# Local masked scores on alternating PSUM banks with the mask laid a unit ahead, local products on one bank, routing weights stored by one DMA

## The reference, cut to what matters

```python
x = L0_attn_x                                   # (8, 1024, 256)
xn = _layernorm(x)
return x + attn(xn) + ffn(xn)
# attn: 16 heads of 16; heads 0-3 causal ("global"), heads 4-15 causal inside a
#       window of 64 ("local"): scores, -inf where masked, softmax, times v, out projection
# ffn:  two branches (fwd, inv), each 8 experts of rank 64:
xV = einsum('btd,kdr->btkr', Q_side, V);  cum_yW = cumsum(einsum('btd,kdr->btkr', K_side, W))
weights = softmax(gelu(Q_side @ router_w1.T + b1) @ router_w2.T + b2 + expert_bias)
out = einsum('btkr,kdr->btd', xV * cum_yW * weights[..., None], U) + weights @ b
```

## Time and profile before, and how to read them

| | us |
|---|---|
| median of 3 runs | 1487.91 (1486.12 to 1490.52) |
| the profiled execution's own time | 1491.34 |
| its span | 1489.6 |
| PE busy | 1379.5 (93%) |
| DVE busy | 989.5 (66%) |
| ACT busy | 776.1 (52%) |
| POOL busy | 586.5 (39%) |

### The profile page before, as it was taken

One profiled execution on the slowest core, in us unless ns is written; L12 is line 12 of the kernel. 1 busy time (PEld: TensorE's weight loads), 2 busy tenths in 40 slices (PEclk: granted clock), 3 DMA queues, 4 the chain that ended last, 5 costly groups with the idle time before them and its releaser, 6 DMA issues.

```text
span 1489.6 us, 35980 instructions
## 1 busy us (share of the span) xinstructions
PE 1379.5 (93%) x14481; PEld 1035.7 (70%) x14481; DVE 989.5 (66%) x2082; ACT 776.1 (52%) x1368; POOL 586.5 (39%) x663
## 2 busy tenths in 40 slices
PE   5978999999999999999999999999999999999996
PEld 4567685777758677586856778587775868667773
DVE  6667777567756777557875677566875578656661
ACT  2434537455464735645374554646356453755544
POOL 1025343453514444253433525144452534335341
PEclk9999999999999999999999999999999999999998
DMA  8430625326062541616353171624516153431610
GB/s 189 102 94 11 168 79 127 105 65 174 25 175 70 121 126 49 166 32 151 96 123 107 40 196 30 158 87 107 141 42 163 44 146 100 118 109 42 172 40 15
DMA packets 166614, 152.88 MB, mean 103 GB/s; under 512 B 37809, under 2 KB 149808, under 8 KB 166448
## 3 DMA queue, kind: packets, MB, share of 16 engines
q1 hardware_dynamic: 166448, 150.59, 38.8%
HBM read 108.57 MB, written 35.65 MB: 97 GB/s over the span
## 4 chain that ended last, share of the span: by engine, by line
PE 62%; DVE 15%; ACT 8%; issue 6%; DMA 4%; POOL 2%; SPq 1%; ACTq 0%; POOLq 0%; DVEq 0%
PE PS L676 30%; PE PS L787 11%; PE PS L821 4%; DVE rest L1193 3%; PE PS L880 3%; ACT HE L1063 3%; PE PS L807 3%; PE PS L909 3%; PE PS L898 2%; PE PS L963 2%; DMA weights_d<-weights_t 2%; DVE area L1198 2%; DVE area L1196 2%; ACT HE L1055 2%; ACT PS L1048 1%
## 5 line engine op out<-in xcount | busy, mean ns | idle before, releaser
L1504 POOL TENSOR_TENSOR PL<-prod,PH 128x512 fp32r<-128x512 f32 x128 | 164.7, 1287 | 201.3 <-ACT PH L1037 201.3
L676 PE MATMUL PS<-XH,WH 128*128 128x512 f32 x512 | 218.6, 427 | 21.7 <-ACT prod L1027 10.3
L1037 ACT ACTIVATE PH<-prod 128x512 fp32r<-128x512 f32 x128 | 80.8, 632 | 268.8 <-DVE prod L1305 252.8
L1499 POOL TENSOR_TENSOR prod<-prod,rest 128x512 f32<-128x512 f32 x96 | 124.8, 1303 | 242.9 <-DMA rest<-weights_d 166.6
L1229 DVE TENSOR_REDUCE block_peak<-PS 128x4 f32<-128x512 f32 x288 | 179.8, 685 | 48.0 <-PE PS L821 47.9
L676 PE MATMUL PS<-XH,WL 128*128 128x512 f32 x512 | 204.1, 399 | 0.0
L676 PE MATMUL PS<-XL,WH 128*128 128x512 f32 x512 | 203.6, 398 | 0.0
L1482 POOL TENSOR_SCALAR_AFFINE_SELECT HE<-HE 128x256 f32<-128x256 f32 x128 | 51.2, 406 | 364.2 <-ACT HE L1063 360.6
L1063 ACT ACTIVATE HE<-PS 128x512 f32<-128x512 f32 (+1 forms) x320 | 159.9, 553 | 33.5 <-PE PS L880 30.5
L1305 DVE TENSOR_TENSOR prod<-PS,prod 128x512 f32<-128x512 f32 x128 | 87.8, 686 | 97.3 <-PE PS L676 84.5
L676 PEld LDWEIGHTS PS<-XH,WH 128*128 128x128 f32 x512 | 97.1, 190 | 63.2 <-ACT prod L1027 16.8
(11 more groups left out here) (186 smaller groups left out, 3064.6 us busy)
## 6 DMA issues: line engine op xcount, KB each, us to landing
parts_d<-area SPq DMA_DIRECT2D x32, 768.0 KB, 5.0
area<-parts_d SPq DMA_DIRECT2D x128, 192.0 KB, 7.9
rest<-weights_d SPq DMA_DIRECT2D x192, 128.0 KB, 3.0
area<-parts_d SPq DMA_DIRECT2D x32, 576.0 KB, 7.8
tok<-in_L_attn_x_dram SPq DMA_DIRECT2D x16, 512.0 KB, 6.2
xt<-in_L_attn_x_dram SPq DMA_DIRECT2D x16, 512.0 KB, 4.1
wide<-weights_d SPq DMA_DIRECT2D x64, 128.0 KB, 3.0
out_dram<-xt SPq DMA_DIRECT2D x16, 512.0 KB, 3.8
```

Source lines behind the costliest of these rows:

```text
L676: ins = e.matmul(ps, a, b, start=first and k == 0, stop=last and k == n - 1, skip_group_check=True)
L1037: e.activation(PH[:, h, :], prod[:, j % 3, :], ACT.Copy).then_inc(phi)
L1499: e.tensor_tensor(prod[:, j % 3, :], prod[:, j % 3, :], wide[j % WIDE], ALU.mult).then_inc(weighed)
L1504: e.tensor_tensor(PL[:, j % 2, :], prod[:, j % 3, :], PH[:, j % 2, :].bitcast(F32), ALU.subtract).then_inc(plo)
```

## The change

It does five things:

1. All three local groups put their products on bank 7 (`ctx_bank`).
2. Pair 0 of every local unit uses bank 5; pair 1 alternates banks 6 and 4.
3. The seed of the next unit's pair 1 stands ahead of this unit's scores, and the first unit's pair 1 is seeded too: its seed is placed before the last two expert groups (in the last chunk before the two groups ahead of the four that belong to the local stretch). The mask matmul L835 is then not used.
4. The peak blocks are woven over two expert groups fewer.
5. `weights_t` is stored whole, 128 rows of 1 KB, with one DMA in place of four of 8 rows; a wide row is then read back as two pieces of 1 KB instead of one of 2 KB.

```diff
     def ctx_bank(grp):
-        return 7 if grp % 2 else 4
+        return 7 if grp else 4
...
         units = [(grp, half) for grp in range(1, 1 + NL // 4) for half in range(2)]
-        scores = [(ch, grp, half, pair, score_use()) for grp, half in units for pair in range(2)]
+        scores = [(ch, grp, half, pair, f"bank{6 - 2 * (n % 2) if pair else 5}") for n, (grp, half) in enumerate(units) for pair in range(2)]
+        masks = [[(add_seed, bank, "lscore", *key)] for *key, bank in scores[1::2]]
         order = []
         for n, (grp, half) in enumerate(units):
-            order.append([(add_lscore, *scores[2 * n]), (add_lscore, *scores[2 * n + 1])])
-            if n + 1 < len(units):
-                order[-1].append((add_seed, scores[2 * n + 3][4], "lscore", *scores[2 * n + 3][:4]))
+            order.append(masks[n + 1] if n + 1 < len(units) else [])
+            order[-1] = order[-1] + [(add_lscore, *scores[2 * n]), (add_lscore, *scores[2 * n + 1])]
             if n:
                 order[-1].append((add_lav, ch, *units[n - 1]))
-        return order
+        return order, masks[0]
...
         run(experts[0] + peaks[0])
-        weave(experts[1:split], peaks[1:])
+        weave(experts[1:split - 2], peaks[1:])
+        locals_, first_mask = local_groups(ch)
+        for group in [first_mask] + experts[split - 2:split]:
+            run(group)
...
-        weave(local_groups(ch), side)
+        weave(locals_, side)
...
-        weights_d = nc.dram_tensor("weights_d", (2 * KE, C), F32, kind="Internal").ap()
+        weights_d = nc.dram_tensor("weights_d", (P, HALF), F32, kind="Internal").ap()
...
-                    for w in range(2):
-                        for h in range(2):
-                            row = 32 * (2 * w + h)
-                            e.dma_start(weights_d[KE * w:KE * (w + 1), h * HALF:(h + 1) * HALF], weights_t[row:row + KE, :]).then_inc(weights_out, 16)
+                    e.dma_start(weights_d, weights_t[:, :]).then_inc(weights_out, 16)
...
+                    by_half = weights_d[2 * 32 * (j // KB):2 * 32 * (j // KB + 1), :].rearrange("(h e) t -> e h t", h=2)
                     for k in range(2):
-                        e.dma_start(wide[j % WIDE][R * k:R * (k + 1), :], weights_d[2 * j + k:2 * j + k + 1, :].to_broadcast([R, C])).then_inc(wide_in[j % WIDE], 16)
+                        n = 2 * (j % KB) + k
+                        e.dma_start(wide[j % WIDE][R * k:R * (k + 1), :].rearrange("p (h t) -> p h t", h=2), by_half[n:n + 1].to_broadcast([R, 2, HALF])).then_inc(wide_in[j % WIDE], 16)
```

More of the change, by code:

```diff
@@ L1290, in vector_program @@
                     q.wait_step()
-                    q.wait_ge(weights_out, 16 * 4 * ch)
+                    q.wait_ge(weights_out, 16 * ch)
                     q.wait_ge(rows_cast, ch)
@@ L1648, in sync_program @@
                     ch, j = key
-                    q.wait_ge(weights_out, 16 * 4 * (ch + 1))
+                    q.wait_ge(weights_out, 16 * (ch + 1))
                     if j >= WIDE:
```

## The result

The changed kernel takes **1511.2 us** (median of 4 runs, 1506.4 to 1514.6) against 1487.0 (4 runs, 1484.0 to 1490.5) for the kernel before, measured beside it: a ratio of 1.016, 95% interval 1.0123 to 1.0196. Slower was forecast; 1507 was the number, and 1511 lies inside the range. The medians are 24.2 apart where 19.2 was forecast; the profiled executions are 19.2 apart. The sum was right in size, but not all of its terms were, and the work behind the result was to find out which.

What follows compares the result with a forecast made beforehand. PE was 93% busy, but ACT, then DVE, paced the local stretch, whose delays reach the end. Even chunks 8.4 us, odd 11.2, last chunk +0.4, chunk 0 -0.8: +19.2 on 1487.9 gives 1507, range 1488 to 1517.

Steps and rivals of the forecast that it cites:

- The second wait: Local stretch: PE's product of group 3 waits on bank 7 for DVE's transpose of group 2, 1.6 us.
- Covered by the +0.2: Local stretch: group 2's wait for group 1's transpose falls within the 0.2 us by which unit 2's product moves in even chunks.
- bank 7's term: Local stretch: sharing bank 7 delays hidden 1 by 1.0 us (even), 0.8 (odd), and DVE by 0.55 in even chunks.
- The removed waits pay nothing: Local stretch: removing PE's mask-seed waits, 0.8 us per chunk, gains nothing on the path; the POOL select is late next.
- Rival 1: Local stretch: bank 7 is free in time or PE has other work, so removed masks and waits gain: about 1473 us; chance 0.1.
- Peak blocks two groups earlier: Last product before the local stretch comes 0.7 us earlier in odd chunks, taking back the 0.57 of ACT's extra seed.
- In even chunks the blocks stay three groups apart: 0: Expert stretch: weaving peak blocks over fewer groups costs even chunks 0, against +0.8 us in each of 7 odd chunks.
- the -0.8 of the issues: Chunk 0: three fewer DMA issues on SP ahead of the first wide save 0.8 us, once.
- The weights: Way into the next chunk after even chunks: 0.45 us for more bytes plus 0.05 for 1 KB pieces, sum 0.5.
- Rival 2: Second bank wait stays but terms cancel: 0.2 to 0.5 us per even chunk, nothing in odd, 1488 to 1492; chance 0.14.
- Rival 3: Weights landing follows the number of DMAs: one store gains 0.9 us per even chunk, 11 less in all, 1496; chance 0.12.
- Rival 4: Moved DVE and POOL operations overlap anew, 0.4 us twice per chunk, 12 on top: 1519; chance 0.1.

Runs made afterwards that it cites:

- e1: Kernel before with only the bank changed: all three local groups' products on bank 7; 1514.22 us, ratio 1.0176.
- e9: Kernel before with groups 1 and 2 on bank 7, group 3 on bank 4, hidden 2 on bank 7; 1497.56 us, ratio 1.0068.
- e7: Changed kernel with weights edits undone and peak blocks over all groups again except in chunk 15: masks ahead and bank 7; 1517.42 us, ratio 1.0201.
- e10: e7 with products of units 2 and 4 behind the first parts stage, peak blocks two groups fewer in chunk 0 and odd chunks; 1489.99 us, ratio 1.0017.
- e12: Kernel before with products of units 2 and 4 moved behind a parts stage on PE, plus e8's weave; 1480.4 us, ratio 0.9955.
- e8: Kernel before with peak blocks two expert groups fewer only in chunk 0 and odd chunks up to 13; 1480.3 us, ratio 0.9952.
- e3: Kernel before with both weights edits: one DMA storing weights_t, wides read in 1 KB pieces; 1493.59 us, ratio 1.004.
- e4: Kernel before with four weight stores kept but laid out as half rows, so wides come in 1 KB pieces; 1492.18 us, ratio 1.0016.
- e5: Changed kernel with group 3's products back on bank 4, hidden 2 on bank 7, last unit's pair 1 on bank 6; 1496.48 us, ratio 1.006.
- e6: e5 with weights as before the change and the weave two groups fewer only in chunk 0 and odd chunks; 1492.88 us, ratio 1.0042.

## Why the prediction was right, and where its steps were not

- **The sign and its cause: right.** The products on bank 7 decide, through DVE's transposes: both waits are in the trace, 30 times in 15 chunks, and e1 by itself brings the loss. The second wait was put at 1.6, with +0.2 at 1.8 in even chunks: the product of group 3 came 2.16 later in chunk 6 and 1.55 in chunk 7, though in chunk 7 only 0.66 of it is this wait, since PE comes to it late. Hidden 1 started 19.60 behind the first local score and starts 20.97, +1.4 where +1.0 was forecast.
- **"Covered by the +0.2", the first wait: wrong.** The terms were nearly right: transpose 0.33 earlier (0.4), product 0.34 later (0.2). What failed is that this is harmless. By itself (e9) it adds 0.4 to each local stretch without any dip, since what follows on PE feeds the DVE steps that set the end, and with the dips 10 us in all. No term of the sum had the clock. The trace of before shows it at 1.00 in every local stretch up to chunk 14, and nothing there said that it would fall once PE stood 0.5 to 1.1 us more.
- **The size of bank 7's term.** This is the term that was sized worst: it entered the sum with 0.55 in 8 even chunks (through DVE and the queue) and 0.8 in 7 odd ones, 10 us. e1 shows 26 for bank 7 alone, some 1.25 per chunk without a dip and the dips on top. In the whole change it is less, +16.2 over the local stretches of chunks 1 to 14 (28 in e1), because the weave takes 1.0 back in odd ones and only two of the seven even ones have a dip, against six in e1.
- **"The removed waits pay nothing": right**, by e7 and by e10 against e12. Rival 1 is out, in both its forms: the waits on the transposes are there, and giving PE other work in them (e10) only brings the kernel back to the time of before.
- **"Peak blocks two groups earlier", -0.7 in odd chunks: right in kind, too small (-0.98).** I let it cancel against the seed's 0.57. Expert stretch of odd chunks +0.8: right for chunks 3 and 7 (+0.76), a little high for the others (+0.6), and the forecast sign is there: PE's waits on the seeds of the maxima (L1043, after it L1046) went from 4 to 17. **"In even chunks the blocks stay three groups apart: 0": wrong**, +0.6, since the chain of maxima is earlier on DVE and in front of a product.
- **Chunk 0: the -0.8 of the issues was right (start -0.8), but what matters was missed**: with other maxima in its weave its expert stretch went from 40.40 to 34.68. That is the one gain in the change, and e8 is made of it.
- **The weights.** 0.5 per even chunk was forecast. By themselves 0.33 (e3, barely clear of the spread), but inside the change nothing: the last stretch is 20.57 as before. Of the sign to look for: from `weights_t` to the issue of the first wide the seven even chunks have 5.6 on the mean (6.2 before), where some 6 was forecast and a microsecond less would have been wrong. The wide pieces were sized at 0.05 with an upper end of 0.3; they land 0.5 later and cost 0.5 per even chunk by themselves (e4). The first multiplication with a wide waited for the DMA before and waits for ACT's copy after, POOL's timeline at the start of chunk 7, before then after:

```profile
703.36 2.84 POOL L1499 TENSOR_TENSOR prod<-prod,rest 128x512 f32<-128x512 f32 x2 [5.94 <-DMA rest<-weights_d]
```

```profile
709.95 1.29 POOL L1502 TENSOR_TENSOR prod<-prod,rest 128x512 f32<-128x512 f32 x1 [6.27 <-ACT prod L1030]
...
711.87 1.29 POOL L1502 TENSOR_TENSOR prod<-prod,rest 128x512 f32<-128x512 f32 x1 [0.63 <-DMA rest<-weights_d]
```

- **The sum** came out right by luck in part, by terms that offset each other: even chunks 1.93 each (forecast 1.05), odd chunks 1.25 (1.6), chunk 0 -3.0 (+1.05), the last +0.8 (0.4), the start -0.8 (-0.8). In the profiled pair that is +19.2, as forecast; the medians differ by 24, of which 5 is that the profiled run of before lies 4.3 above its median and that of after 0.7 below.
- **Rival 2**, the terms cancel: out. The local stretch grew by 1.27 and 0.68 in chunks 6 and 7, and the expert stretch won nothing back.
- **Rival 3**, coalescing: at most 0.17 per even chunk (e4 to e3), within the spread, not 0.9. **Rival 4**, new meetings of operations: its 1519 wasn't reached, but what it named is there: the cast of 1.21 beside POOL in even chunks, in another stretch than it had in mind.

Open: what decides whether the clock falls (e9's chunks 3 and 7); whether masks ahead would pay with the scores' banks as before; whether one store with wides in 2 KB pieces would gain anything. No kernel was made for these three.

## What to carry to other kernels

Before two results share a bank, look at what stands ahead of the evacuation of the first on its engine, and price the wait at both ends: what PE misses, and which late engine is fed by what PE does next. A wait that nothing needs is worth nothing removed; one added where PE runs from one short piece of work to the next may also lower its clock. Take a change of several parts apart before keeping or dropping it: here one part, used in 8 of 16 chunks, made the kernel 0.5% faster while the whole made it 1.6% slower.

## What the runs showed of the hardware that was not expected

- The granted clock falls to the 1.2 GHz level for 3.4 us in the middle of work, after two short stands of PE (0.53 and 1.13 in chunk 7 after, 0.71 and 0.76 in e9). With the same work around it, that goes with 0.6 to 0.8 more for the local stretch in e9, about 0.4 to 0.5 in e5 and e6, 0.5 to 1.1 in e1 (only 0.1 in chunk 2 after), and with 1.5 where it comes 17 us in; always less than half of 3.4, as the stretch is not PE's alone. It does not follow from the work ahead of it alone: chunk 6 after stood 0.97 and 2.30 and has none, nor has e9's chunk 7.
- A DMA of 128 KB that copies one row to many partitions lands in 3.0 us in pieces of 2 KB and in 3.5 in pieces of 1 KB (3.4 in the whole change), the bytes being the same. The two pieces of a row also lie 32 KB apart in DRAM; size and distance were not told apart.
- A cast of 128x128 on DVE took 0.23 us in one place of the order and 1.21 two expert groups earlier, where an operation of POOL was running when it began and ended 0.09 us before it (644.02 to 645.23, POOL to 645.14); in all 36 slow ones of the 448 in the 14 traces POOL was at work at the start, in none of the others.
